# One 512-column add per step instead of two of 256, in the convolution of a graph network

## The reference, cut to what matters

```
src = node_in[edge_src];  s0 = src[:, :64];  s1 = src[:, 64:] as (3 x 64)
out0 = alpha * ((s0 * a0) @ w_00_0 + inv_sqrt3 * sum_m(s1[m] * a1[m]) @ w_11_0)
out1 = alpha * ((s0 * a1[m]) @ w_01_1 + (s1[m] * a0) @ w_10_1)      for m = 0, 1, 2
messages = concat(out0, out1) * radial(edge)
agg = segment_sum(messages, edge_dst)
```

## Time and profile before

| | us |
|---|---|
| median of 3 runs | 2801.38 |
| the profiled execution | 2804.37 |
| its span, first to last instruction | 2802.7 |
| VectorE busy in the span | 1928.9 |
| first gather of the convolution issued at | 1564.42 |
| last add of the convolution | about 2142 |

### The profile page before, as it was taken

One profiled execution on the slowest core, in us unless ns is written; L12 is line 12 of the kernel. 1 busy time (PEld: TensorE's weight loads), 2 busy tenths in 40 slices (PEclk: granted clock), 3 DMA queues, 4 the chain that ended last, 5 costly groups with the idle time before them and its releaser, 6 DMA issues. The chain is left out here.

```text
span 2802.7 us, 41395 instructions
## 1 busy us (share of the span) xinstructions
PE 2206.6 (79%) x11128; PEld 1477.4 (53%) x11128; DVE 1928.9 (69%) x4009; ACT 1409.5 (50%) x4483; POOL 1585.7 (57%) x1695
## 2 busy tenths in 40 slices
PE   6996777777777756869996687877878699999774
PEld 3544555555555545746652433333335687788763
DVE  4565999999999888811117899999997433323787
ACT  2221655566655634511126599999996322222242
POOL 2645666666666212667677777777775177777000
PEclk9998888888888875579996899999999589999998
DMA  3214667666667110313323333333331311111005
GB/s 110 59 46 129 203 200 211 201 198 194 207 202 203 36 62 21 104 50 109 110 66 101 108 104 105 104 104 103 104 105 38 89 31 39 39 39 34 14 1 196
DMA packets 167619, 292.87 MB, mean 104 GB/s; under 512 B 53832, under 2 KB 101965, under 8 KB 167398
## 3 DMA queue, kind: packets, MB, share of 16 engines
q0 software_dynamic: 77520, 186.78, 24.0%
q1 hardware_dynamic: 80720, 87.10, 9.9%
q10 hardware_dynamic: 9158, 16.33, 1.6%
HBM read 253.35 MB, written 36.75 MB: 104 GB/s over the span
## 5 line engine op out<-in xcount | busy, mean ns | idle before, releaser
L2499 PE MATMUL cv_ps<-cv_msg,cv_hot 128*128 128x512 f32 x880 | 421.4, 615 | 116.1 <-DVE acc L2561 84.4
L2486 POOL DMA_INDIRECT cv_x<-x_tab,e_src x440 | 425.8, 968 | 139.8 <-issue 92.6
L2517 ACT ACTIVATE cv_msg<-cv_x,factors 128x64 f32<-128x64 f32 x1320 | 357.8, 336 | 0.0
L2912 POOL DMA_INDIRECT gs_h<-h_tab,fc_q x280 | 264.4, 944 | 155.4 <-issue 82.8
L657 POOL DMA_INDIRECT at_kv_tail<-kv_tab,e_src x272 | 264.7, 973 | 149.5 <-PE at_a L1136 76.2
L2499 PEld LDWEIGHTS cv_ps<-cv_msg,cv_hot 128*128 128x128 f32 x880 | 159.6, 194 | 342.1 <-ACT cv_msg L2517 170.8
L2076 POOL DMA_INDIRECT pairs<-gating_pair,gating_place x256 | 251.9, 984 | 125.5 <-issue 62.2
L2561 DVE TENSOR_TENSOR acc<-acc,cv_ps 128x256 f32 x880 | 308.9, 416 | 8.9 <-PE cv_ps L2499 5.5
L1111 PE MATMUL at_q<-q_parts,at_hot_n 128*128 x1320 | 228.4, 329 | 41.4 <-DVE at_kv_head L1208 17.2
L2514 ACT ACTIVATE cv_msg<-cv_x,factors 128x256 f32<-128x256 f32 x440 | 218.4, 496 | 18.0 <-DMA cv_x<-x_tab,e_src 17.9
L2866 ACT ACTIVATE gs_x_hid<-gs_x_h,x_b 128x128 f32<-128x128 f32 x320 | 91.2, 368 | 270.5 <-PE gs_x_h L2833 270.5
(11 more groups left out here) (571 smaller groups left out, 4710.8 us busy)
## 6 DMA issues: line engine op xcount, KB each, us to landing
x_space<-in_L_ffn_w SPq DMA_DIRECT2D x16, 1024.0 KB
at_rel_row<-e_rel_rows SPq DMA_DIRECT2D x55, 256.0 KB, 4.2
experts_out<-gs_y ACTq DMA_DIRECT2D x20, 512.0 KB
x_y<-experts_out SPq DMA_DIRECT2D x20, 512.0 KB, 8.0
cv_x<-x_tab,e_src POOLq DMA_INDIRECT x440, 2.7
kv_tab<-p_qkv SPq DMA_DIRECT2D x25, 256.0 KB, 2.0
gs_h<-h_tab,fc_q POOLq DMA_INDIRECT x280, 2.3
at_kv_tail<-kv_tab,e_src POOLq DMA_INDIRECT x272, 3.8
```

The lines of the kernel that those rows point to most:

```text
L2486: nc.gpsimd.indirect_dma_start(out=xg[:, i % RT, u, :], out_offset=None, in_=x_tab, in_offset=bass.IndirectOffsetOnAxis(ap=e.src[:, t:t + ...
L2499: nc.tensor.matmul(ps[u % R][:, :], hot[:, i % 2, u, :], msg[:, i % 2, u, :], start=True, stop=True).then_inc(summed, 1)
L2517: ins = nc.scalar.activation(parts[:, 1, 1 + m], xg[:, i % RT, u, 0:M], ACT.Copy, scale=factor[:, t:t + 1, 1 + m])
L2912: nc.gpsimd.indirect_dma_start(out=hg[:, i % RT, u, :], out_offset=None, in_=h_tab, in_offset=bass.IndirectOffsetOnAxis(ap=e.src[:, i * U ...
```

## The change

Per step one add of 512 columns instead of two of 256. `added` then counts steps and not halves. TensorE's wait for step t-4 means the same as before. VectorE's own wait is now `added >= t`.

```
-                            pe.wait_ge(added, 2 * (t - R) + 2)
+                            pe.wait_ge(added, t - R + 1)
```

```
                         dve.wait_ge(summed, t + 1)
-                        for n in range(2):
-                            if t:
-                                dve.wait_ge(added, 2 * t + n - 1)
-                            row = acc[:, ds(b, 1), n * D:(n + 1) * D].rearrange("p a w -> p (a w)")
-                            v.tensor_tensor(row, row, ps[u % R][:, n * D:(n + 1) * D], ALU.add).then_inc(added, 1)
+                        if t:
+                            dve.wait_ge(added, t)
+                        row = acc[:, ds(b, 1), :].rearrange("p a w -> p (a w)")
+                        v.tensor_tensor(row, row, ps[u % R][:, :], ALU.add).then_inc(added, 1)
```

```
-                dve.wait_ge(added, 2 * T1)
+                dve.wait_ge(added, T1)
```

## The result

The changed kernel takes 2824.12 us (median of 5 runs, 2821.1 to 2833.27), the kernel before beside it 2802.84 us (5 runs, 2801.19 to 2807.85). The ratio is 1.0083, with a 95% interval of 1.0066 to 1.0100: 21 us by the medians, 18 to 28 by the interval. The forecast was 2820.3 us.

What follows compares the result with a forecast made beforehand. GpSimd's gathers bound the convolution before, VectorE after. Terms 17.2 (52 turns) + 1.2 (end) + 0.5 (short stalls) = 18.9 us gave 2823.3 for the profiled execution, 2820.3 us for the median; range 2805 to 2831.

Steps and rivals of the forecast that it cites:

- GpSimd sets the pace before: Convolution stage before the change: GpSimd issues a gather every 1.272 us, 10.17 us a turn; VectorE has 0.35 us room.
- A wide add costs 0.60 alone and 0.89 behind an add: VectorE's 512-column add: pitch 0.60 us unhindered, 0.89 with a 0.21 us stall behind another add, five stalls a turn.
- The turn: VectorE's turn after the change: 10.40 us, 10.50 with node adds and covered stalls, above GpSimd's 10.17.
- It decides at a stall of 0.14: Stall between neighbouring adds on VectorE: below 0.14 us nothing changes, above it each 0.01 costs 2.5 us.
- The end of the stage: From the last weigh to the convolution's end, VectorE takes 16.2 us instead of 15.03, +1.2 us.
- 52 turns cost 17.2 us more and stray stalls 0.5: Third to last weigh: 52 turns of 10.50 instead of 10.17 us, +17.2; seven short stalls of other origin, +0.5.
- a low clock only as a rival: Much slower: TensorE's clock falls at times, such turns take 13.3 us; one turn in ten gives 2834 us; chance 0.05.
- Everything behind only starts later: All stages after the convolution are shifted by the same amount, otherwise unchanged.
- GpSimd waits above 0.3 us for its ring: Expected sign in the changed profile: GpSimd shows waits above 0.3 us for ScalarE or VectorE.
- The rule of the Trainium skill: Advice to minimize operations, not semaphores, said to cost nothing; leads to the no-change rival, 2801 us, chance 0.12.

Runs made afterwards that it cites:

- 5: Kernel before with the gathers of the odd steps left out from turn 4 on: 2778.30 us, ratio 0.9905.
- 6: Changed kernel with the gathers of the odd steps left out from turn 4 on: 2828.17 us, ratio 1.0087.
- Number 3: Changed kernel with the two waits ahead of an add swapped in the code, `added` first, then `summed`: 2803.60 us, ratio 1.0005.
- number 1: Kernel before, adds still two of 256 columns, but each waits for all adds before it: 2956.74 us, ratio 1.0575.
- number 2: Changed kernel, turns 0 to 48 wait for all adds but the newest, odd steps add two blocks further on: 2801.93 us, ratio 0.9997.
- second trace: Both kernels run unchanged once more for another trace: 2812.29 us before the change, 2829.19 us after, one run each.
- 11: Kernel before with only its join moved apart: add 1, first half of join, add 2, second half, adds 3 to 7: 2794.35 us, ratio 0.9958.
- 7: Changed kernel with swapped waits (`added` before `summed`) and the join's two operations moved apart between adds 1, 2 and 3: 2800.43 us, ratio 0.9989.
- 4: Changed kernel with the join's two operations moved apart between adds 1, 2 and 3: 2807.21 us, ratio 1.0012.
- 12: Kernel before, join moved apart, adds 0 to 2 of 512 columns, adds 3 to 7 in halves with loose wait: 2795.57 us, ratio 0.9966.

## Why the prediction was right, and where not

- *GpSimd sets the pace before.* Right: numbers 5 and 6.
- *A wide add costs 0.60 alone and 0.89 behind an add.* Right to 0.01 us. The page counts 249 stalls of 52.9 us behind an add, and 22 more whose matmul was also awaited; forecast were 250 to 270 with about 55 us.
- *The turn.* 10.40 forecast, 10.42 measured.
- *It decides at a stall of 0.14.* Number 3 has exactly this stall and is level with the kernel before; number 1 shows the wait alone, number 2 its absence.
- *The end of the stage.* 16.2 us forecast from the last weigh, 16.3 measured (2154.31 to 2170.62).
- *52 turns cost 17.2 us more and stray stalls 0.5.* This term was mis-sized: the 52 turns grew by 25.8 us in the first pair of traces, 22.6 in the second. Regular turns make 52 x 10.42 + 24 x 0.33 - 9 x 0.29 = 547 us, 18 us more than before; the other 8 us are long turns, 4 us in the second trace: about 5.3 and 2.1 us in turns 15, 28 and 41, behind TensorE's wait for a node add, and 7 x 0.35 = 2.5 us of fixed pauses. The kernel before had long turns too, four over 11 us in each trace, but gathers went on through them, and VectorE made up for them in the turns behind, most of them 9.4 to 9.8 us. With VectorE as the bound each is paid in full. I had priced a low clock only as a rival that would have to become more frequent. In the 52 turns it fell 4 and 4 times before and 3 and 5 times after; it became dearer at about the same frequency. The rival's price of such a turn, 13.3 us, was right: turns 15 and 28 of the first trace took 13.02 and 13.41. TensorE's wait for node adds is in no term of the forecast, and the seven pauses were taken for 0.5 us.
- *Everything behind only starts later.* The stages behind were 9 and 8 us shorter in the two pairs. Over all fourteen traces they take 651 to 667 us, and the length goes with the granted clock: the eight traces at 0.89 or 0.90 take 651 to 659, the six at 0.87 or 0.88 take 659 to 667. That the change has a part in it is not shown. This shortening hides the miss of the term above: the stage cost 24 to 27 us against 18.9 forecast, the program 21. That 2820.3 came within 4 us of 2824.12 is in part luck.
- *GpSimd waits above 0.3 us for its ring.* Wrong. Its list shows 0.3 us as the longest, and its last gather starts at 2130.20, 24 us ahead of the last weigh. VectorE's weigh stood 3.9 us behind the last gather of its turn at the start of the stretch and 24.1 at its end, 0.39 us a turn (0.31 in the second trace); the ring of four turns is never full before the stage ends.
- *The rule of the Trainium skill* ("VectorE: DVE Perf Modes"), that the semaphore costs nothing, doesn't hold for these adds: number 1 adds only waits, and costs 155 us.

## What to carry to other kernels

Two half-width operations on disjoint columns are not only one operation cut in two: each half is the distance that lets the next one be prepared before its neighbour is done. Before merging operations, count what the merged one has to wait for, and look for a pair in the trace that already runs that way. If a wait on the neighbour can't be avoided, put other work between the two, or write the wait that ends last ahead of the other in the code, as number 3 does, so that it is carried by the instruction nearest the operation. And an engine with 0.35 us of room in 10 is next in line: from there on small stalls that cost nothing are paid in full.

## What the runs showed that I had not expected

- The order of two waits in the code is worth 0.07 us each time the second is the late one: pitch 0.83 against 0.89, some 20 us in this kernel by the medians.
- At seven fixed turns there are 0.35 us more ahead of an add, in three of them between its register operation and the add. The kernel before has seven such pauses too, 0.23 us each; it had room for them, the changed one has not.
- Gathers are issued faster with the join's two operations apart: 551.7, 553.3, 553.5 and 555.2 us from first to last issue (numbers 11, 7, 4 and 12) against 558.6 twice in the kernel before, with 2, 9, 12 and 12 against 21 and 18 gathers more than 1.5 us after the last. Number 2 shows that it isn't the place of the join alone: its join is together, and it has 555.1 us and 10. The traces show where the slow ones are. Every gather recorded at over 1.0 us runs beside an operation of the join, in all fourteen traces: 36 in the kernel before, 42 in the changed one, 10 in number 11. Others beside it take the usual 0.95. One of them, in the kernel before, with the operations of the join beside it:

```profile
1803.05 0.69 DVE L2549 TENSOR_TENSOR cv_msg<-cv_s1w 128x512 f32<-128x512 f32 x1
...
1803.23 1.32 POOL L2486 DMA_INDIRECT cv_x<-x_tab,e_src  x1 [0.30 <-ACT cv_msg L2517]
...
1803.77 0.69 DVE L2551 TENSOR_TENSOR cv_msg<-cv_msg,cv_s1w 128x512 f32<-128x512 f32 x1
```

The join's operations read two tensors from SBUF; that this is the cause was not tried.
